# Layer 0 of a four-layer residual kernel: from quarter products on quadrants to whole products of 128 rows, in a block amid each convolution

## The reference, cut to what matters

```python
def _L0_cond_ref(x, embedding, W0, b0, W1, b1, W2, b2, weight, bias_k):   # L2, L3 alike
    h = jax.nn.gelu(embedding @ W0 + b0, approximate=False)
    h = jax.nn.gelu(h @ W1 + b1, approximate=False)
    att = jax.nn.softmax((h @ W2 + b2) / T, axis=-1)
    agg_w = jnp.einsum('bk,koi->boi', att, weight[..., 0])
    agg_b = att @ bias_k
    return jnp.einsum('boi,bih->boh', agg_w, x) + agg_b[:, :, None]

def _L1_cond_ref(x, c, weight, c_weight, bias):
    out = lax.conv_general_dilated(x, weight, window_strides=(1,), padding=[(4, 4)],
                                   dimension_numbers=('NCH', 'OIH', 'NCH'), feature_group_count=4)
    return out + jnp.einsum('nd,od->no', c, c_weight)[:, :, None] + bias[None, :, None]

x = x + _L0_cond_ref(x, cond_128, ...)
x = x + _L1_cond_ref(x, cond_128, L1_cond_weight, L1_cond_c_weight, fside_S_0)
x = x + _L2_cond_ref(x, cond_128, ...)
x = x + _L3_cond_ref(x, cond_128, ...)
```

## Time and profile before

| | before |
|---|---|
| median of 3 runs | 494.14 us (492.7 to 495.86) |
| the profiled execution, whole | 493.25 us |
| its span (first to last instruction) | 491.5 us |
| PE / PEld busy | 98% / 97% |
| DVE, ACT, POOL busy | 69%, 57%, 31% |
| DMA | 93.01 MB, 189 GB/s |
| granted TensorE clock, mean | 0.994 of full |

### The profile page before, as it was taken

One profiled execution on the slowest core, in us unless ns is written; L12 is line 12 of the kernel. 1 busy time (PEld: TensorE's weight loads), 2 busy tenths in 40 slices (PEclk: granted clock), 3 DMA queues, 4 the chain that ended last, 5 costly groups with the idle time before them and its releaser, 6 DMA issues.

```text
span 491.5 us, 17843 instructions
## 1 busy us (share of the span) xinstructions
PE 481.1 (98%) x7966; PEld 477.0 (97%) x7966; DVE 338.2 (69%) x415; ACT 279.1 (57%) x417; POOL 152.4 (31%) x148
## 2 busy tenths in 40 slices
PE   6999999999999999999999999999999999999995
PEld 5988999999999999999999999999999999999995
DVE  2846976766777666767887676767876676777423
ACT  5843466555555666555655665555556665556444
POOL 3835341333233151334133142333224133430110
PEclk9998999999999999999999999999999999999998
DMA  8687776566566775465656756565677746452124
GB/s 289 255 298 225 227 212 203 147 183 189 165 204 210 215 214 181 134 200 156 203 209 216 214 179 189 145 197 179 195 216 215 212 144 223 129 191 65 77 88 172
DMA packets 38252, 93.01 MB, mean 189 GB/s; under 512 B 3856, under 2 KB 24600, under 8 KB 34208
## 3 DMA queue, kind: packets, MB, share of 16 engines
q1 hardware_dynamic: 38176, 91.86, 59.9%
HBM read 54.10 MB, written 37.75 MB: 187 GB/s over the span
## 4 chain that ended last, share of the span: by engine, by line
PE 95%; DVE 2%; DMA 1%; issue 1%; ACT 0%; SPq 0%; POOL 0%; DVEq 0%; ACTq 0%
PE cv_ps L481 56%; PE aux_ps L461 18%; PE aux_ps L504 16%; PE cv_ps L409 1%; DMA consts_sb<-in_consts_dram 1%; PE cv_ps L422 1%; PE cv_ps L504 1%; PE aux_ps L409 1%; DVE x_lo L745 0%; DVE x_lo L732 0%; PE aux_ps L432 0%; DVE x_hi L739 0%; PE aux_ps L395 0%; DVE y_all L818 0%; PE aux_ps L380 0%
## 5 line engine op out<-in xcount | busy, mean ns | idle before, releaser
L481 PE MATMUL cv_ps<-x_hi,conv_lo 32*128 32x512 f32 x1536 | 254.4, 391 | 0.0
L481 PE MATMUL cv_ps<-x_lo,conv_hi 32*128 32x512 f32 x1536 | 254.4, 391 | 0.0
L481 PE MATMUL cv_ps<-x_hi,conv_hi 32*128 32x512 f32 x1536 | 253.4, 390 | 0.0
L752 DVE SCALAR_TENSOR_TENSOR x_lo<-cv_ps,d_all,x_hi 128x512 fp32r<-128x512 f32 x128 | 93.5, 751 | 121.8 <-ACT x_hi L605 121.8
L615 ACT ACTIVATE y_all<-aux_ps,e_all 128x512 f32<-128x512 f32 x124 | 83.7, 690 | 124.1 <-PE aux_ps L504 120.6
L481 PEld LDWEIGHTS cv_ps<-x_hi,conv_hi 32*128 32x128 f32 x1536 | 136.7, 184 | 0.0
L481 PEld LDWEIGHTS cv_ps<-x_hi,conv_lo 32*128 32x128 f32 x1536 | 136.4, 184 | 0.0
L481 PEld LDWEIGHTS cv_ps<-x_lo,conv_hi 32*128 32x128 f32 x1536 | 136.2, 184 | 0.0
L605 ACT ACTIVATE x_hi<-cv_ps,d_all 128x512 fp32r<-128x512 f32 x128 | 88.3, 690 | 58.2 <-PE cv_ps L481 54.8
L461 PE MATMUL aux_ps<-x_hi,a_hi 32*128 32x512 f32 x512 | 98.1, 395 | 0.9 <-DVE x_lo L732 0.9
L745 DVE SCALAR_TENSOR_TENSOR x_lo<-aux_ps,c_all,x_hi 128x512 fp32r<-128x512 f32 x128 | 91.6, 749 | 9.2 <-ACT x_hi L599 9.0
(11 more groups left out here) (119 smaller groups left out, 490.0 us busy)
## 6 DMA issues: line engine op xcount, KB each, us to landing
x_sb<-in_x_dram SPq DMA_DIRECT2D x31, 1024.0 KB, 6.5
out_dram<-y_all SPq DMA_DIRECT2D x62, 512.0 KB, 7.5
a_rep<-a_pairs SPq DMA_DIRECT2D x64, 128.0 KB, 7.2
m_rep<-m_pairs SPq DMA_DIRECT2D x64, 128.0 KB, 7.0
a_pairs<-a_all SPq DMA_DIRECT2D x1, 1920.0 KB, 8.9
m_pairs<-m_all SPq DMA_DIRECT2D x1, 1792.0 KB, 11.8
m_all<-in_mix_dram SPq DMA_DIRECT2D x3, 512.0 KB, 6.0
x_sb<-in_x_dram SPq DMA_DIRECT2D x2, 512.0 KB, 7.7
```

Of the source, the lines that this page charges most:

```text
L481: mm = pe.matmul(cv_ps[:, g, :], w[rows(g), j, :], a[n % 2][rows(g), q, s:s + T], start=(i == 0), stop=(i == steps - 1))
L752: nc.vector.scalar_tensor_tensor(x2_lo[n % 2][:, g, :], cv_ps[:, g, :], d_all[:, n, g:g + 1], x2_hi[n % 2][:, g, :].bitcast(F32), ALU.add, ...
```

## The change

Layer 0 no longer works on quadrants. The input is laid out in natural channel order with its four phases along the free dimension (the stage's output layout is the same as before). A phase is now three matmuls of 128 rows and 512 columns, twelve for a batch in place of 48 of 32 rows. They are no steps of the lanes: `layer0(n+1)` is issued as one block, when lane 0 has done 18 of the 36 steps of the convolution of n. The out product of n-1 follows the whole convolution of n.

Because no copy per quadrant is needed, `a0_pairs`, `a0_rep`, its saves and its replicating DMAs are gone, and POOL splits straight from `a0_all` in 128x128 pieces. `bias2_rows` gets a buffer of its own. DVE's `split_x` of a second half stands behind `x2_out`, and its wait on `l0_done` lets each half go as soon as the two phases that read it are done. ACT and DVE do `x1_out(n+1)` before `x2_out(n)`. At the start, DVE copies `e_all` before it splits batch 1, and the convolution of batch 0 waits for `m_out` lane by lane.

```diff
-        x_sb = two("x_sb", [P, G, T])
+        x_sb = two("x_sb", [P, PH, T])
-        a0_hi = two("a0_hi", [P, G, P], F32R)
-        a0_lo = two("a0_lo", [P, G, P], F32R)
+        a0_hi = two("a0_hi", [P, P], F32R)
+        a0_lo = two("a0_lo", [P, P], F32R)
-        a0_rep = sb("a0_rep", [P, 2, G, PAIR, P])
+        bias2_rows = sb("bias2_rows", [K, NOG, P])
...
-            def replicate_a0(pair, phases):
-                if pair < B // PAIR:
-                    sp.wait_ge(a0_saved[min(pair, 1)], DMA)
-                    wait(sp, a0_split, 2 * PAIR * (pair - 1))
-                    replicate(a0_dram, a0_rep, a0_rep_loaded, pair, phases)
...
             load(1)
-
-            sp.wait_ge(mix_out_v, ROUNDS)
-            sp.wait_ge(mix_out_a, ROUNDS)
-            save(a0_all, a0_dram, 0, 1, a0_saved[0])
-            replicate_a0(0, range(PH))
-            save(a0_all, a0_dram, 1, B // PAIR, a0_saved[1])
             load(2)
-
-            sp.wait_ge(c_made, 1)
-            replicate_a0(1, range(PH))
...
-                replicate_a0(n // 2 + 2, part)
                 replicate_m(n // 2 + 1, part)
...
-            def layer0_steps(n, p):
+            def layer0(n):
...
                 pe.wait_ge(a0_split, 2 * (n + 1))
-
-                wait(pe, y_out, PH * (n - 3) + p + 1)
-                i, steps = 0, 3 * G
-                for g in range(G):
-                    h = g // PER
-                    if g % PER == 0:
+                for p in range(PH):
+                    h = p // PER
+                    if p % PER == 0:
                         pe.wait_ge(x_lo_done, HALVES * n + h + 1)
-                    for w, a in ((a0_hi, x_hi), (a0_lo, x_hi), (a0_hi, x_lo)):
-                        mm = pe.matmul(aux_ps[:, p, :], w[n % 2][rows(p), g, :], a[h][rows(p), g % PER, :],
-                                       start=(i == 0), stop=(i == steps - 1))
-                        i += 1
-                        if i == steps:
-                            mm.then_inc(l0_done, 1)
-                        yield
+
+                    wait(pe, y_out, PH * (n - 3) + p + 1)
+                    for k, (w, a) in enumerate(((a0_hi, x_hi), (a0_lo, x_hi), (a0_hi, x_lo))):
+                        mm = pe.matmul(aux_ps[:, p, :], w[n % 2][:], a[h][:, p % PER, :], start=(k == 0), stop=(k == 2))
+                    mm.then_inc(l0_done, 1)
...
-                if n == 0 and g == 0:
-                    pe.wait_ge(conv_split, 2)
-                    pe.wait_ge(zero_cols, 4)
-                    pe.wait_ge(m_out, B // QUAD)
-                    pe.wait_ge(e_out, 1)
+                if n == 0:
+                    if g == 0:
+                        pe.wait_ge(conv_split, 2)
+                        pe.wait_ge(zero_cols, 4)
+
+                    if g == 1:
+                        pe.wait_ge(e_out, 1)
+                    else:
+                        pe.wait_ge(m_out, B // QUAD - (2, 0, 1, 0)[g])
...
                 for n in range(B - 1):
-                    yield from layer0_steps(n + 1, g)
                     conv = conv_steps(n, g)
-                    if 0 < n < B - 2:
-                        yield from itertools.islice(conv, CONV_A)
+                    yield from itertools.islice(conv, CONV_A)
+                    if g == 0:
+
+                        layer0(n + 1)
+                    yield from conv
+                    if n > 0:
                         yield from out_steps(n - 1, g)
-                    yield from conv
-
-                yield from out_steps(B - 3, g)
+
...
-            in_turn([layer0_steps(0, p) for p in range(PH)])
+            layer0(0)
...
             for n in range(B):
-                if 0 < n:
-                    x2_out(n - 1)
                 if n + 1 < B:
                     x1_out(n + 1)
-                if n == 1:
-                    act.wait_ge(e_out, 1)
-                if 0 < n < B - 2:
+                x2_out(n)
+                if n > 0:
                     evacuate_y(n - 1)
...
             def split_a0(n):
-                pair = n // PAIR
-                src = a0_rep[:, pair % 2, :, n % PAIR, :]
-                pool.wait_ge(a0_rep_loaded[pair % 2], DMA * PH * (pair // 2 + 1))
+                if n == 0:
+                    pool.wait_ge(mix_out_v, ROUNDS)
+                    pool.wait_ge(mix_out_a, ROUNDS)
+                src = a0_all[:, n, :]
...
-                wait(dve, l0_done, PH * n)
+                wait(dve, l0_done, PH * (n - 1) + PER * (h + 1))
...
             x1_out(0)
+            dve.wait_ge(e_made, 1)
+            nc.vector.tensor_copy(e_all[:], e_ps).then_inc(e_out, 1)
             split_x(1, 0)
             split_x(1, 1)
-            dve.wait_ge(e_made, 1)
-            nc.vector.tensor_copy(e_all[:], e_ps).then_inc(e_out, 1)
-            for n in range(B + 1):
-                if 0 < n:
-                    x2_out(n - 1)
+            for n in range(B):
                 if n + 1 < B:
                     x1_out(n + 1)
                 if n + 2 < B:
                     split_x(n + 2, 0)
+                x2_out(n)
+                if n + 2 < B:
                     split_x(n + 2, 1)
...
-        "x": a["x"].reshape(B, G, CG, T, PH).transpose(0, 4, 2, 1, 3).reshape(B, P, G, T),
+        "x": a["x"].reshape(B, P, T, PH).transpose(0, 1, 3, 2),
```

More of the change, by code:

```diff
@@ L107, in cond_resid_kernel @@
         fside_sb, eye32_sb = consts_sb[:, P + OG + HO:P + OG + HO + G], consts_sb[:, P + OG + HO + G:]
-        a0_dram = nc.dram_tensor("a0_pairs", [B // PAIR, P, PAIR * P], F32).ap()
         m_dram = nc.dram_tensor("m_pairs", [B // PAIR, P, PAIR * P], F32).ap()
@@ L142, in cond_resid_kernel @@
             "p (g m) -> p g m", g=NOG)[:, :, 0:OG] for n in range(NL)]
-        bias2_rows = by_og(a0_rep[:].rearrange("p s g k m -> p (s g k m)"), NOG * P)[0:K]
         rep_flat = m_rep[:].rearrange("p s g k m -> p (s g k m)")
@@ L178, in cond_resid_kernel @@
         x_first = [sem(f"x_first{j}") for j in range(2)]
-        a0_rep_loaded = [sem(f"a0_rep_loaded{j}") for j in range(2)]
         m_rep_loaded = [sem(f"m_rep_loaded{j}") for j in range(2)]
         stored = [sem(f"stored{j}") for j in range(YBUFS)]
-        a0_saved = [sem(f"a0_saved{j}") for j in range(2)]
         m_saved = [sem(f"m_saved{j}") for j in range(2)]
@@ L319, in _ @@
             sp.dma_start(conv_f[:], conv).then_inc(conv_loaded, DMA)
-            sp.dma_start(bias2_rows, bias[:, NL * P:].rearrange("k (g m) -> k g m", g=NOG)).then_inc(e_loaded, DMA)
+            sp.dma_start(bias2_rows[:], bias[:, NL * P:].rearrange("k (g m) -> k g m", g=NOG)).then_inc(e_loaded, DMA)
             sp.dma_start(w3_sb, w3).then_inc(e_loaded, DMA)
             load(1)
-            sp.wait_ge(mix_out_v, ROUNDS)
-            sp.wait_ge(mix_out_a, ROUNDS)
-            save(a0_all, a0_dram, 0, 1, a0_saved[0])
-            replicate_a0(0, range(PH))
-            save(a0_all, a0_dram, 1, B // PAIR, a0_saved[1])
             load(2)
-            sp.wait_ge(c_made, 1)
-            replicate_a0(1, range(PH))
             sp.wait_ge(m_out, 1)
@@ L442, in bias_e @@
                 return mm
-            def layer0_steps(n, p):
-                if n == 0 and p == 0:
+            def layer0(n):
+                if n == 0:
                     pe.wait_ge(spread_lo[NL - 1], 1)
@@ L634, in _ @@
                 m_evacuate(m)
+            act.wait_ge(e_out, 1)
             for n in range(B):
-                if 0 < n:
-                    x2_out(n - 1)
                 if n + 1 < B:
                     x1_out(n + 1)
-                if n == 1:
-                    act.wait_ge(e_out, 1)
-                if 0 < n < B - 2:
+                x2_out(n)
+                if n > 0:
                     evacuate_y(n - 1)
-            evacuate_y(B - 3)
-            x2_out(B - 1)
-            evacuate_y(B - 2)
             evacuate_y(B - 1, range(0, PH, 2))
```

## The result

The changed kernel takes 516.76 us (median of 6), the one before 493.32 beside it: a ratio of 1.0458, interval 1.0431 to 1.0485. It is 4.6% slower. I had forecast 497.6 with a range to 503.5; the time is far outside. The profiled execution has 516.37 us against 493.25, 23.1 more.

A forecast was written before the change was run, and what follows sets the result against it. TensorE was taken as the bound, by length and number of its slots. Blocks +7.1, start -0.57, idle time -0.87 and slow clock -1.70 gave +4.0 us on 493.25; forecast 497.6, range 490.5 to 503.5.

The forecast's parts named there:

- Pace: Layer 0 in steady batches: a whole product takes 0.218 us against a 0.2322 slot, gaining 0.17 us per batch.
- whole products are no faster: Rival, 20%: layer 0's whole products keep the slot's pace; +9.4 us, about 503.
- The forecast's period: Steady part: layer 0 of consecutive batches begins 14.16 us apart, against 13.93 before.
- Switch: TensorE between quarter and whole products: 0.10 drain plus 0.10 bare load, twice per batch, 0.40 us.
- the rival built on it: Rival, 17%: loads are hidden at TensorE's switches between quarter and whole products; -2.2 us, about 491.5.
- So nothing new is on the path: these edits cost 0: Other engines in steady batches: ACT, DVE, POOL and SP keep up with TensorE, so 0 us is added.
- DVE comes late: Rival, 7%: lane 0 waits for x2's low part or the third phase for x; 0.5 us per batch, 513.
- the forecast's 1.1 us: Smallest slack in a steady batch: DVE's low part for lane 0 is done 1.1 us before its next convolution.
- The start: Program start: layer 0 of batch 0 as whole products saves 0.57 us; idle time and slow clock go too.
- The idle 0.87 and the 1.70 of slow clock: TensorE's wait for x of batch 1 near 40 us and the clock fall after it vanish: -0.87 and -1.70 us.
- Sum: Whole kernel: 7.1 - 0.57 - 0.87 - 1.70 = +4.0 us on 493.25, stated as 497.6.
- Sign: Whole kernel, 1% margin: within 0.52, slower (above 499.1 us) 0.39, faster (below 489.2 us) 0.09.

The follow-up runs named there:

- e3: e1 with each whole product of 512 columns cut into two of 256 columns; 508.26 us (two runs).
- e6: e1 with all whole products of layer 0 reading one fixed bf16 matrix and one fixed bf16 block; 496.17 us, ratio 1.0077.
- e1: The changed kernel with 8 empty steps per lane between the convolutions of batches 0 and 1; 506.38 us, ratio 1.0257.
- e2: e1 with the block of twelve whole products cut into two of six, three slots of quarter products apart; 517.49 us (two runs).
- e7: The kernel before (quarter products) in the changed kernel's order, plus the 8 empty steps of e1; 499.91 us, ratio 1.0119.
- e9: The kernel before, unchanged, in its third profile; 493.0 us.

## Why the prediction was wrong, point by point

- **Pace (failed).** I priced a whole product at 0.218, a quarter of the slot's excess, for a gain of 0.17 per batch. It is 0.2323; the gain is nothing. The trace had the two-sided bounds, and I chose the wrong end: two 256-column matmuls on the same rows cost only 0.008 more than one of 512, which I read as a price per instruction. The same two rows also allow a small fixed cost and a larger one per column, and that is what e3 finds (0.004 and 0.015). e6 shows that the part per column goes with the fp32r operands, as far as its fixed operands can show it. The Trainium skill ("TensorE: Matmul & The Clock Gate", Part 1) gives 215.7 ns for 512 columns; bf16 agrees with it (215.5 in e6), fp32r does not (232 in e1). My rival "whole products are no faster" had the right pace for the wrong reason. The forecast's period was 0.14 short: 0.17 by the pace and 0.02 by the switches, less the 0.05 that the quarter slots gave back. Worth: 31 x 0.14 = 4.4 us.
- **Switch (held).** 0.20 per switch was forecast, 0.21 measured in e2, half of it a load that nothing hides. Waits that are already met do not explain that load: none stands between the block and the slot after it, and the step behind that slot is as long; and the out product, which has waits of its own, starts at 204.32 and goes on at 204.56 without a long step. The Trainium skill ("TensorE: Matmul & The Clock Gate", Part 2) says that TensorE pulls loads ahead to the background buffer or to other row groups; at the switch the trace does not agree, and the rival built on it falls. The Trainium skill ("TensorEngine Tiling (Array Packing)", Key Properties) says that a change of tiling mode drains TensorE; the trace agrees, and the drain is half of the price.
- **"So nothing new is on the path: these edits cost 0" (failed).** The slack was worked out for a batch with an out product between two convolutions. I did not walk the first batch, where there is none: 11.5 us, as much as all 31 blocks together, and a term that the order of instructions would have shown. It is neither pace nor switch, but four turns of ACT 0.70, DVE 0.76 and the issue, and the clock that falls on them. The rival "DVE comes late" had the semaphore, but in every batch and by way of a slower DVE, and that did not happen. The a0 traffic that I put at 8 MB each way was 10.7 MB in all (93.01 MB before, 82.35 after); taking it out gained nothing that shows.
- **In the steady part the slack did hold**: TensorE waits for nothing after 64 us in the changed kernel. Lane 0's low part is done at about 206.0 (four in 2.86 from 205.24) and its next convolution starts at 207.06, the forecast's 1.1 us:

```profile
205.24 2.86 DVE L727 SCALAR_TENSOR_TENSOR x_lo<-cv_ps,d_all,x_hi 128x512 fp32r<-128x512 f32 x4 [1.78 <-ACT x_hi L584]
207.06 0.39 PE L459 MATMUL cv_ps<-x_hi,conv_hi 32*128 32x512 f32 x1
```

- **The start (failed in part).** -0.57 for layer 0 of batch 0 was -0.4 at most. From 31.80 to 40.88 it is 9.08 us, before 9.29, but the drain in front of it is saved too: e1, at full clock, has 10.89 us from the block before it to the convolution (27.10 to 37.99), the kernel before 11.27 (26.74 to 38.01). What is missing is mainly the pace, 0.17. And the first product is followed after 0.31 us (28.91, 29.22 in e1) though both sides of it have 128 rows: its load isn't hidden either, which I had put at nothing. The idle 0.87 and the 1.70 of slow clock were in one of three profiles only; the medians hold neither as a gain.
- **Sum.** The blocks and the boundary alone are 11.5 + 11.5 = 23.0 us, and the medians lie 23.4 apart. So close a match is in part luck: the slow clock at 25 us (about 3 us) weighs on most runs of the changed kernel and on few of the kernel before.
- **Sign.** The sum was +4.0 and the time rose, but the chance of a clear loss, 0.39, was too low, and the range stopped 13 us short. No rival had the boundary.

What stays open: what brings the slow clock at 25 us in some executions, which fp32r operand sets the pace, and why the quarter slots between the blocks take 0.2311. No version tried is faster than the kernel before beyond its interval.

## What to carry to other kernels

Four quarter products side by side ran at the pace of one whole product (0.2322 and 0.2323 us), so turning one into the other gained nothing by itself, while every change between the two cost 0.2 us on TensorE here; count the changes first. When the order of stages is rotated, walk the first and the last round: a stage that covers a wait in the steady part may not exist there, and a few waits in a row cost twice, once as idle time and once as slow clock (here 5.6 us and 5.9 us). A stretch of slow clock in a single profile should be seen in a second one before its removal is counted.

## What the runs showed of the hardware that was not expected

At full granted clock a product of 512 columns started 0.232 to 0.233 us after the last in fp32r, whether of 128 rows or as four of 32 rows at once, and 0.2155 us in bf16 (e6). Two of 256 columns took 0.237 (e3). The load in front of the first product behind a switch cost 0.10 us in fp32r and 0.02 in bf16, with the drain of 0.10 unchanged. That load was bare, too, in front of the first whole product of the program (0.08 us, e1), where the products before it had 128 rows as well. In the changed kernel the granted clock fell right behind the first of the four waits, 1.65 us to 54.32 (0.85 over 54 to 56 us, then 0.50 to 68); in e7 it fell behind a single one of 1.62 us (0.50 from 56 to 60 us, 0.94 from 60 to 64); after the 0.3 us of e9 it stayed at 1.00. It also fell at 25 us, in 5 of 13 profiles, with TensorE busy all the time.
